# Output products of a fused attention and feed-forward kernel: from fp32 to three fp32r terms with streamed weights, and three masked heads on ScalarE

## The reference

```python
q = (hidden_states @ Wq).reshape(b, t, 2, H, RET // 2)
sim = jnp.einsum('btphn,hkpn->pbthk', q, keys)
...
scores, pk = jax.lax.top_k(all_sc, KPH)
...
de = down_embed[idx]
ue = up_embed[idx]
w = jnp.einsum('btd,bthkd->bthk', hidden_states, de)
w = jax.nn.silu(w) * jax.nn.softmax(scores, axis=-1)
experts_states = jnp.einsum('bthk,bthkd->btd', w, ue)
mlp = jax.nn.silu(hidden_states @ Wg + bg) * (hidden_states @ Wu + bu) @ Wd + bd
return mlp + experts_states
```

## Time and profile before

| | |
|---|---|
| time, median of 3 runs | 3519.4 us (3515.91 to 3520.86) |
| the profiled execution | 3515.04 us, span 3513.3 us |
| TensorE busy | 3414.6 us, 97% of the span |
| VectorE, ScalarE, GpSimd busy | 2830.2, 1990.0, 1163.0 us |
| granted TensorE clock, mean | 0.991 |

### The profile page before, as it was taken

How to read it: one execution, slowest core, us unless ns; L and a number is a source line. 1 busy time by engine, 2 the same in 40 slices (tenths; PEclk the granted TensorE clock), 3 DMA queues, 4 the chain that set the end, 5 groups by cost and what they waited for, 6 DMA issues and landing times.

```text
span 3513.3 us, 49408 instructions
## 1 busy us (share of the span) xinstructions
PE 3414.6 (97%) x18400; PEld 2693.9 (77%) x18400; DVE 2830.2 (81%) x5316; ACT 1990.0 (57%) x2886; POOL 1163.0 (33%) x724
## 2 busy tenths in 40 slices
PE   8779999999999999999999999999999999999988
PEld 6457877777877777877777877777777778777777
DVE  4688888888888888888888887888878888888873
ACT  4456556555566555556555655555655564555551
POOL 0233333333333333333333333333333333343330
PEclk9899999999999999999999999999999999999999
DMA  4000000000000000000000000000000000000000
GB/s 121 18 13 19 7 13 19 19 19 19 7 13 19 19 19 14 12 13 19 19 19 9 17 13 19 19 19 7 19 13 19 19 13 7 13 13 7 12 7 12
DMA packets 23452, 60.84 MB, mean 17 GB/s; under 512 B 5808, under 2 KB 10160, under 8 KB 23216
## 3 DMA queue, kind: packets, MB, share of 16 engines
q1 hardware_dynamic: 23216, 57.69, 5.0%
HBM read 40.91 MB, written 16.78 MB: 16 GB/s over the span
## 4 chain that ended last, share of the span: by engine, by line
PE 81%; DVE 8%; ACT 6%; issue 3%; POOL 2%; DMA 0%; SPq 0%; POOLq 0%; DVEq 0%; ACTq 0%
PE ring L651 25%; PE y_bank L744 11%; PE y_bank L746 10%; PE step_bank L553 6%; PE step_bank L545 5%; PE step_bank L651 4%; PE step_bank L589 3%; PE step_bank L581 3%; PE step_bank L680 3%; DVE prob L1144 3%; PE step_bank L670 3%; PE step_bank L724 3%; PE step_bank L539 2%; POOL grid L464 2%; PE y_bank L740 1%
## 5 line engine op out<-in xcount | busy, mean ns | idle before, releaser
L464 POOL TENSOR_TENSOR grid<-ex 128x1024 f32<-128x1024 f32 x512 | 997.6, 1956 | 1507.5 <-ACT ex L877 730.6
L744 PE MATMUL y_bank<-wd_sb,gate 128*128 128x256 f32 x2048 | 622.3, 386 | 1.7 <-DVE wexp L1166 1.7
L746 PE MATMUL y_bank<-up_sb,wexp 128*128 128x256 f32 x2048 | 609.1, 379 | 0.0
L1144 DVE SCALAR_TENSOR_TENSOR prob<-grid,narrow,prob 128x1024 f32<-128x1024 f32 x256 | 552.2, 2157 | 9.0
L651 PE MATMUL ring<-x1T_hl,downT_hl 128*128 128x512 f32 x1536 | 420.8, 409 | 16.8 <-ACT gate L901 16.7
L651 PE MATMUL ring<-x1T_hl,wg_hl 128*128 128x512 f32 x1536 | 431.2, 416 | 3.8 <-DVE gate L1160 3.8
L1131 DVE SCALAR_TENSOR_TENSOR grid<-grid,best 128x1024 f32<-128x1024 f32 x256 | 327.2, 1278 | 131.8 <-POOL grid L464 128.8
L746 PEld LDWEIGHTS y_bank<-up_sb,wexp 128*128 128x128 f32 x2048 | 389.2, 190 | 53.0
L651 PE MATMUL ring<-x1T_hl,wu_hl 128*128 128x512 f32 x1536 | 421.4, 409 | 0.0
L744 PEld LDWEIGHTS y_bank<-wd_sb,gate 128*128 128x128 f32 x2048 | 354.0, 190 | 53.3 <-issue 25.2
L651 PEld LDWEIGHTS ring<-x1T_hl,wu_hl 128*128 128x128 f32 x1536 | 282.0, 188 | 119.8 <-issue 42.9
(11 more groups left out here) (169 smaller groups left out, 5578.7 us busy)
## 6 DMA issues: line engine op xcount, KB each, us to landing
xb<-in_L_attn_x SPq DMA_DIRECT2D x34, 512.0 KB, 3.5
out_y<-x SPq DMA_DIRECT2D x32, 512.0 KB, 2.9
xa<-in_L_attn_x SPq DMA_DIRECT2D x30, 512.0 KB, 4.2
prob<-in_L_ffn_down_embed SPq DMA_DIRECT2D x1, 1024.0 KB, 6.0
prob<-in_L_ffn_Wg SPq DMA_DIRECT2D x1, 1024.0 KB, 8.8
prob<-in_L_ffn_Wu SPq DMA_DIRECT2D x1, 1024.0 KB, 10.9
wd_sb<-in_L_ffn_Wd SPq DMA_DIRECT2D x1, 1024.0 KB, 11.3
up_sb<-in_L_ffn_up_embed SPq DMA_DIRECT2D x1, 1024.0 KB, 11.8
```

Of the source, the lines that this page charges most:

```text
L464: pool.tensor_tensor(grid[:, h % 2], bcast(ex[:, h, 0:NX].unsqueeze(2), [P, NX, NK]), bcast(ex[:, RH + h, 0:NK].unsqueeze(1), [P, NX, NK]) ...
L744: pe.matmul(rows, gate[:, c % 2, t * P:(t + 1) * P], wd_sb[:, c, :], start=(c == 0 and t % 2 == 0), stop=False, skip_group_check=True)
L746: mm = pe.matmul(rows, wexp[:, c % 2, t * P:(t + 1) * P], up_sb[:, c, :], start=False, stop=(c == C - 1), skip_group_check=True)
L1144: ins = dve.scalar_tensor_tensor(out=row, in0=g, scalar=rz[:, h:h + 1], in1=row, op0=ALU.mult, op1=ALU.add, accum_out=mass[:, 0:1] if h == ...
```

## The change

Each operand of the two output products is split into a high part (rounded to fp32r) and a low part (the rest): high by high, high by low and low by high make three fp32r matmuls in place of one fp32 matmul.

- *Weights.* `wd_sb` and `up_sb`, which lay in SBUF, are gone. In the fill eight parts (four of `Wd`, four of `up_embed`) are cast by ScalarE, their low parts made by VectorE, and stored by SyncE in a DRAM tensor `wdup_kept`. From there GpSimd's queue issues one load of 512 KB per step into one of two halves of `wdup`.
- *Activations.* `gate` and `wexp` now lie in rows of `prob` that are free at the time. ScalarE casts their high parts (`gate_top`, `wexp_top`), VectorE subtracts for the low parts (`ff_low`, by `low`); TensorE waits for `gate_split`, `wexp_split` and `wdup_loaded`. The low part of `wexp` of step `c` is made in VectorE's step `c + 1`, behind `ff_h(c + 1)` (in the last step at its end).
- *Heads.* ScalarE masks heads 0 to 2; VectorE keeps only head 3, adds head 2 by a plain addition, and does this add behind `keep(t, 3)`.

```diff
@@ -46,7 +46,7 @@
...
-    ACT_HEADS, STEEP = 2, float(2 ** 30)
+    ACT_HEADS, STEEP = 3, float(2 ** 30)
@@ -87,7 +87,8 @@
...
-        wd_sb, up_sb = sb("wd_sb", P, C, D), sb("up_sb", P, C, D)
+        wdup = sb("wdup", P, 2, 4, D, dt=F32R)
+        wdup_kept = nc.dram_tensor("wdup_kept", [C, P, 4, D], F32).ap()
@@ -119,20 +120,31 @@
...
-        drop, lift = narrow[:, 10:12], narrow[:, 12:14]
+        drop, lift = narrow[:, 10:13], narrow[:, 13:16]
...
-        gate = sb("gate", P, 2, G)
-        wexp = sb("wexp", P, 2, G)
+        gate_hi, gate_lo = sb("gate_hi", P, 2, G, dt=F32R), sb("gate_lo", P, 2, G, dt=F32R)
+        wexp_hi, wexp_lo = sb("wexp_hi", P, 2, G, dt=F32R), sb("wexp_lo", P, 2, G, dt=F32R)
+        def gate(par, c):
+            return prob[:, 1 - par, 2 + c % 2, G:] if c < C // 2 else prob[:, par, c % 2, 0:G]
+        def wexp(par, c):
+            return prob[:, 1 - par, 2 + c % 2, 0:G] if c < C // 2 else prob[:, par, 2 + c % 2, 0:G]
@@ -345,9 +364,11 @@
-        PREP_STEPS, PREP_WG, PREP_WU = 11, 9, 10
+        PREP_STEPS, PREP_WG, PREP_WU = 18, 9, 10
+        PREP_WD = {11: (0,), 12: (1,), 13: (2,), 14: (3,)}
+        PREP_UP = {14: (0,), 15: (1,), 16: (2,), 17: (3,)}
@@ -370,7 +391,7 @@
-            for dst, src in ((wq_sb, Wq), (wo_sb, Wo), (wd_sb, Wd), (up_sb, up)):
+            for dst, src in ((wq_sb, Wq), (wo_sb, Wo)):
@@ -380,6 +401,14 @@
+            sp.wait_ge(prep_full, 4)
+            sp.dma_start(wd_rows, Wd.rearrange("(c p) n -> p c n", p=P)).then_inc(wd_staged, 16)
+            sp.wait_ge(low_ready, 2)
+            sp.dma_start(up_rows, up.rearrange("(c p) n -> p c n", p=P)).then_inc(up_staged, 16)
+            for w, i in [(0, 0), (0, 1), (0, 2), (0, 3), (1, 0), (1, 1), (1, 2), (1, 3)]:
+                sp.wait_ge((wd_low, up_low)[w], i + 1)
+                sp.dma_start(wdup_kept[2 * i:2 * i + 2, :, 2 * w:2 * w + 2, :].rearrange("c p w d -> p c w d"),
+                             wdup[:, :, 2 * w:2 * w + 2, :].bitcast(F32)).then_inc((wd_kept, up_kept)[w], 16)
@@ -470,9 +499,20 @@
...
+                def ff_stream(c):
+                    g = n * C + c
+                    if g == 0:
+                        pool.wait_ge(wd_kept, 16 * (C // 2))
+                        pool.wait_ge(up_kept, 16 * (C // 2))
+                    wait(pool, y_full, g - 1)
+                    pool.dma_start(wdup[:, c % 2], wdup_kept[c]).then_inc(wdup_loaded[c % 2], 16)
+                    if ff:
+                        ff_stream(c)
@@ -729,8 +769,9 @@
...
                             wait(pe, y_read, n * 2)
-                        pe.wait_ge(h_ready, n * C + c + 1)
-                        pe.wait_ge(*drained("pt", n, c))
+                        pe.wait_ge(wdup_loaded[c % 2], 16 * ((n * C + c) // 2 + 1))
+                        pe.wait_ge(gate_split, n * C + c + 1)
+                        pe.wait_ge(wexp_split, n * C + c + 1)
                     for t in (2 * pair, 2 * pair + 1):
@@ -741,10 +782,11 @@
...
-                        pe.matmul(rows, gate[:, c % 2, t * P:(t + 1) * P], wd_sb[:, c, :],
-                                  start=(c == 0 and t % 2 == 0), stop=False, skip_group_check=True)
-                        mm = pe.matmul(rows, wexp[:, c % 2, t * P:(t + 1) * P], up_sb[:, c, :],
-                                       start=False, stop=(c == C - 1), skip_group_check=True)
+                        terms = [(gate_hi, 0), (gate_hi, 1), (gate_lo, 0), (wexp_hi, 2), (wexp_hi, 3), (wexp_lo, 2)]
+                        for i, (src, w) in enumerate(terms):
+                            mm = pe.matmul(rows, src[:, c % 2, t * P:(t + 1) * P], wdup[:, c % 2, w, :],
+                                           start=(c == 0 and t % 2 == 0 and i == 0), stop=(c == C - 1 and i == 5),
+                                           skip_group_check=True)
@@ -799,6 +841,16 @@
+                for i in PREP_WD.get(k, ()):
+                    act.wait_ge(wd_staged, 16)
+                    wait(act, wd_kept, 16 * i)
+                    act.copy(wdup[:, :, 0, :], wd_rows[:, 2 * i:2 * i + 2, :]).then_inc(wd_high, 1)
...
@@ -887,10 +939,13 @@
...
                     act.wait_ge(spread_ready, s * (RH * T) + t * RH + h + 1)
-                    g = grid[:, h].rearrange("p a b -> p (a b)")
+                    g = grid[:, h % 2].rearrange("p a b -> p (a b)")
                     act.activation(g, g, ACT.Prelu, bias=drop[:, h:h + 1], alpha=STEEP).then_inc(bent, 1)
...
                         act.wait_ge(*full("pt", s - 2, C - 1))
+                        act.wait_ge(wexp_split, (s - 1) * C)
+                    if t == 2 and h == 0 and ff:
+                        act.wait_ge(wexp_split, n * C + C // 2)
                     act.wait_ge(bent, s * (ACT_HEADS * T) + t * ACT_HEADS + h + 1)
@@ -898,12 +953,22 @@
...
                     wait(act, y_full, n * C + c - 1)
+                    if c == 0:
+                        wait(act, wexp_split, n * C)
...
+                def gate_top(c):
+                    act.wait_ge(h_ready, n * C + c + 1)
+                    act.copy(gate_hi[:, c % 2], gate(par, c)).then_inc(gate_high, 1)
+                def wexp_top(c):
+                    act.wait_ge(*drained("pt", n, c))
+                    act.copy(wexp_hi[:, c % 2], wexp(par, c)).then_inc(wexp_high, 1)
@@ -911,6 +976,8 @@
...
                         ff_gate(c)
+                        if c:
+                            wexp_top(c - 1)
                     if at:
@@ -921,11 +988,14 @@
...
                         ff_dots(c)
+                        gate_top(c)
                     if at:
...
                             at_use(*use)
+                    if ff and c == C - 1:
+                        wexp_top(c)
                     if rt and c % 2:
-                        mask(c // 2, 1)
+                        mask(c // 2, 1), mask(c // 2, 2)
                     if rt and c % 2 == 0 and c:
@@ -971,6 +1041,12 @@
+                for i in PREP_WD.get(k, ()):
+                    dve.wait_ge(wd_high, i + 1)
+                    low(wdup[:, :, 1, :], wd_rows[:, 2 * i:2 * i + 2, :], wdup[:, :, 0, :], wd_low)
...
@@ -1137,7 +1213,9 @@
...
-                        dve.wait_ge(masked, s * (ACT_HEADS * T) + t * ACT_HEADS + ACT_HEADS)
+                        dve.wait_ge(masked, s * (ACT_HEADS * T) + t * ACT_HEADS + h + 1)
+                        if h > 1:
+                            rt_steps.wait(marks["add", h - 1])
                         ins = dve.tensor_tensor(row, g, row, ALU.add)
@@ -1157,14 +1235,18 @@
...
+                def ff_low(whole, high_part, low_part, s_high, s_split, c):
+                    dve.wait_ge(s_high, n * C + c + 1)
+                    low(low_part[:, c % 2], whole(par, c), high_part[:, c % 2], s_split)
@@ -1204,20 +1286,26 @@
...
                         ff_h(c)
+                        if c:
+                            ff_low(wexp, wexp_hi, wexp_lo, wexp_high, wexp_split, c - 1)
                     if rt and not odd:
...
                     uses(AT_MID[c])
-                    if rt and odd:
-                        keep(t, 2)
+                    if ff and c == C - 1:
+                        ff_wexp(c)
                     if at and c == 6:
...
                         constants(it // BG - 1)
+                    if ff and c < C - 1:
+                        ff_wexp(c)
                     if ff:
-                        ff_wexp(c)
+                        ff_low(gate, gate_hi, gate_lo, gate_high, gate_split, c)
+                        if c == C - 1:
+                            ff_low(wexp, wexp_hi, wexp_lo, wexp_high, wexp_split, c)
                     if rt and odd:
-                        add_head(t, 1), add_head(t, 2)
+                        add_head(t, 1)
                     uses(KV_LATE[c])
@@ -1232,7 +1320,7 @@
                     if rt and odd:
-                        add_head(t, 3), clamp(t)
+                        add_head(t, 2), add_head(t, 3), clamp(t)
```

More of the change, by code:

```diff
@@ L134, in block_kernel @@
         kp2 = qp[:, 0:2].rearrange("p a n -> p (a n)")
-        v2_sb = gate[:].rearrange("p a n -> p (a n)")[:, 0:2 * FC * VW].rearrange("p (t c w) -> p t c w", t=2, c=FC)
+        v2_at = KD * G + P + 4 * NK
+        v2_sb = grid[:].rearrange("p g a b -> p (g a b)")[:, v2_at:v2_at + 2 * FC * VW].rearrange(
+            "p (t c w) -> p t c w", t=2, c=FC)
         step_bank = [ps(f"step_bank{k}") for k in range(STEP_BANKS)]
@@ L169, in block_kernel @@
         h_ready = sem("h_ready")
+        gate_high, gate_split, wexp_high, wexp_split = (sem("gate_high"), sem("gate_split"),
+                                                        sem("wexp_high"), sem("wexp_split"))
+        wd_staged, wd_high, wd_low, wd_kept = sem("wd_staged"), sem("wd_high"), sem("wd_low"), sem("wd_kept")
+        up_staged, up_high, up_low, up_kept = sem("up_staged"), sem("up_high"), sem("up_low"), sem("up_kept")
+        wdup_loaded = [sem(f"wdup_loaded{k}") for k in range(2)]
```

(36 more changed lines are left out.)

4 lines of the change are left out of this document (2 added, 2 removed).

## The result

The changed kernel takes 3663.1 us (median of four, 3661.8 to 3673.7) against 3518.2 before: ratio 1.0418, 95% interval 1.0397 to 1.0439. The profiled execution is the one of 3673.7 us, 10 above the median.

The account below looks back on a forecast made before the run. TensorE, busy 97%, was taken to bound the kernel, with VectorE just in time in places. 3515 − 156 saved + 26 × 7.35 and 4 × 4.9 of waits + 20 for the fill = 3590, so 3594 median; range 3440 to 3670.

Parts of the forecast that it names:

- likeliest case: Whole kernel: VectorE's late low parts make TensorE wait 7.35 us per full turn; 3594 us, own range 3545 to 3650, chance 0.45.
- TensorE's save: `ff_out` products: three fp32r matmuls replace one fp32 product, 0.61 us less per step, 4.9 per turn, 156 over 256 steps.
- Steps 1 and 2: Chain from the mask of head 1 to wexp's low part: ends 26.85 us in, wanted at 22.5, so TensorE waits 4.35.
- Step 4: Adds, keep, `ff_h` and low part from step 3 end late; TensorE waits 1.3 us (0.7 to 2.4) for wexp's low part.
- Step 7: Low part behind the normalization and `ff_h(7)` ends near 7.3 us, products wanted at 4.97; wait taken as 1.7 us.
- The four drain turns: Turns with no new K/V group: waits taken to eat TensorE's save, 4.9 us each, as ScalarE and VectorE do less.
- The fill: Eight weight parts cast, lowered and stored before the first turn, last low ending at 106.4 us: +20 us (16 to 28).
- VectorE, 92.7 per turn: VectorE's work per full turn: 10.2 us of new subtractions, less four keeps of 1.28, giving 92.7 of then 99.7.
- The shared port: VectorE's new subtractions beside GpSimd's spreads: 5.3 us more VectorE time per turn, 3640; held within the likeliest case's high side.
- VectorE isn't late: Rival: VectorE's early parts move into its idle time, so waits shrink; 3383 us without waits, 3458 with 2.5; faster, chance 0.27.
- The clock: Rival: each 4.35 us gap in step 2 may bring 3.4 us at half speed, 1.7 per turn; 3638 us, chance 0.15.
- The stream: Rival: weight loads on GpSimd's queue come 1 us late in every step; 3850 us, chance 0.05.

Follow-up runs that it names:

- e8: The changed kernel with one swap: VectorE makes wexp's low part of the step before ahead of `ff_h` instead of behind it; 3607.0 us, 1.0254.
- e11: e5 with several low parts, casts and ScalarE's K/V work moved, and the fill's stores on GpSimd's queue with `up` and `Wd` parts interleaved; 3507.9 us, 0.9977.
- e12: e11 without VectorE's low parts of gate and wexp, the third term using the high part again; 3469.4 us, 0.9870.
- e1: The changed kernel with wexp's high and low parts of steps 1, 3, 5 and 6 made within their own step; 3663.5 us, 1.0424.
- e2: The changed kernel without VectorE's two subtractions for the low parts, TensorE taking the high part a second time; 3572.1 us, 1.0163.
- e5: e1 with ScalarE's list reordered: `gate_top` behind its step's attention evictions, the third mask behind the next step's gate; 3532.1 us, 1.0042.

## Why the prediction was right, and where it was off

It said slower at 3594, in 3440 to 3670; it is slower, at 3663. That is 7 us inside the upper end, and above the likeliest case's own range of 3545 to 3650. The direction was reasoned, and the chain in the profile and the swap of e8 bear it out. That the size fell inside the range is partly luck: in the 26 turns two terms that were both too large cancel, and the missing term of the drain was just small enough. (The sum with all upper bounds, given as 3665, adds up to 3663.)

- *TensorE's save, 4.9 per turn*: TensorE's work fell from 104.59 to 100.2 (e11, e12), 4.4. Over the kernel its busy time fell by 77 and not 156; in e12, with the same number of matmuls and less of its time at half speed, by 128. In after's timeline one `gate_lo` matmul begins at 3259.54 and the next, six matmuls on, at 3260.24: 0.117 each, near the 0.119. The 109 ns from the Trainium skill's page (TensorE: Matmul & The Clock Gate, Back-to-back issue gap) is given there for an isolated matmul and not for a stream of weight loads and matmuls, as the prediction took it; this stream does not show it.
- *Steps 1 and 2, wait 4.35*: M and the end of the chain were within 0.3, but only 1.58 us of waiting stand behind that chain; with the 1.12 for the low part of step 0 and the 0.95 for ScalarE's `qp` it is 3.65. *Step 4, 1.3*: 0.84. *Step 7, 1.7*: 1.52. Also 0.47 in step 0. In all 6.5 against 7.35. The 26 turns came to +59 where the sum has 26 × 2.45 = +64, with both parts smaller: 153 us more idle time against 191, 94 us less work against 127. The 192 us before `ff_out` meet the "some 190" by luck: 121 of them lie in the 26 turns.
- *The four drain turns, "I take the waits to eat the save"*: **this term failed.** +16.5 each, 66 of the 84 us by which the profiled execution lies above the sum (3673.7 against 3590). The reason given ("ScalarE and VectorE have less to do there") looks at sums, against the argument's own rule: the mask, keep, add and `ff_h` chain has next to no K/V in it, while TensorE comes sooner. A drain turn's window was there to read: VectorE worked 81.4 of 92.6. Not all of it is waiting: TensorE's busy time in the four turns is 372.5 us, with 68 at half speed, and in e12's 347.2, with 7, so I put the half clock at some 25 of the 66, an estimate. In the last two turns, where the sum has no waits, wexp's low part accounts for 12.
- *The fill, +20*: +29. The last low was forecast at 106.4 and is at 106.44; but the next x load stood behind the eight stores in SyncE's queue, is issued at 108.08, and TensorE waits 9.8 us for it. I had counted the engines that the new steps pass through, and not SyncE's queue. The rows of SyncE's queue (start, us) are these:

```profile
80.64 26.88 SPq L410 DMA_DIRECT2D wdup_kept<-wdup  x8
107.56 0.47 SPq L417 DMA_DIRECT2D xa<-in_L_attn_x  x1
108.08 0.84 SPq L423 DMA_DIRECT2D xb<-in_L_attn_x  x1
```

- *VectorE, 92.7 per turn*: 84.7. The row of 3.03 us was quoted and its cause named, and yet the removed work was priced at 1.28. The shared port cost its new subtractions little: their means are 0.722 and 0.705 against 0.68 alone, 0.5 us per turn in all and not 5.3.
- *ScalarE*: the prediction calls it idle for most of the turn, but its own row has 62.08 us of work in 104.59. The reading hid the engine that e1 and e2 found behind VectorE.
- *Rivals.* "VectorE isn't late" didn't happen. The clock: in the 26 turns with all stages half speed was granted for 31 us (7 before), 1.2 a turn and not the 3.4 of the rival; the wait of 4.35 had come as 1.12, 0.95 and 1.58. In the four drain turns it was granted for 68 us (none before). So the clock did take part where the waits were longest. The stream was in time.
- *The theory behind it* held for the changed kernel (e8), but was half of the cause. e1 shows the other: take VectorE's late part away, and ScalarE, with 18 us more work per turn and casts that wait for VectorE ahead of TensorE's evictions, takes its place. e5 shows that this too was order. What is left in e11, 2.6 us of waits per turn, 25 us more than before in the drain turns and 16 in the fill, is not taken apart by a run; nor is it shown what would bring e12's turn from 101.8 to the 100.2 of TensorE's own work.

## What to carry to other kernels

When a result is put behind a chain on a busy engine, price the chain and not the engine's sum, and do so again for each kind of turn: here the one with less TensorE work had the longest wait. A cast that waits for another engine must not stand ahead of the bottleneck's evictions in an in-order list. And when a wait is removed, look at what stands second on every engine before counting the gain: here 163 us of removed waiting bought nothing until ScalarE's list was changed too.

## What the runs showed of the hardware

- After the 5.54 us pause the products ran at half speed: the identity matmuls above took 1.09 us for four, against 0.63 in the turn of group 13. e1, with pauses of 3.2 us in step 0, has 106 us at half speed in the 26 turns with all stages against 31. In the turn of after shown above, with single pauses of 1.58 us at most, the granted clock was 1.00 in every step.
- The subtraction of two SBUF tiles took 0.68 us, but 1.77 beside a spread. In e1 the low part of wexp runs beside a spread 161 times in 256, after has 31; its mean is 0.945 against 0.705. This agrees with the Trainium skill (SBUF — State Buffer, Who interferes with whom).
- The same section has GpSimd-issued loads starve while VectorE holds the port. The 256 loads landed 3.4 to 5.5 us after their issue (median 3.6), and none is named in TensorE's waits. What VectorE ran at each issue is not taken apart, so this tests the kernel and not the rule.
